# Gated mixing stage: two images at once, one on each half of the partitions

## The chip, the cores and the metric

One core of a Trainium2 chip runs the whole program. The metric is the device time of one execution in microseconds (us), the median of the runs shown. The engines are TensorE (PE; its weight loads are PEld), VectorE (DVE), ScalarE (ACT), GpSimd (POOL) and SyncE (SP), and 16 DMA engines serve the queues of SP, ACT and POOL. All data is fp32.

## The reference

The input x has 8 images of 64 channels and 256x256 pixels. Two layers follow each other, each a group normalisation, an operator and a residual addition. The first layer is the one that is changed here:

```python
def layer0(v, ...):                       # v = _gn(x), 32 groups of 2 channels
    y = einsum('bwhc,dc->bwhd', v, mlp1_w) + mlp1_b
    x1 = _shift1(y[..., :c])              # each quarter of the channels moved by one pixel: up, down, left, right
    x2 = _shift2(y[..., c:2 * c])         # the same with the directions exchanged
    x3 = sigmoid(batchnorm(v) * wbn) * v
    bar = softmax(mlp(sum(x1) + sum(x2)))           # two weights for each image and channel
    out = bar[:, 0] * x1 + bar[:, 1] * x2
    return (einsum('bwhc,dc->bwhd', out, mlp2_w) + mlp2_b) * x3
x = x + layer0(_gn(x), ...)
x = x + spectral(_gn(x), ...)             # 2-D real FFT, 32x32x2 modes mixed by complex 64x64 matrices, inverse FFT
```

## The kernel before

The program runs in stages, one after another. First come the statistics of x (0 to 336 us in the trace) and the preparation of small matrices. Then comes the mixing stage (378 to 1469 us), which computes x1 = x + layer0. A small normalisation step, the forward transform, the mixing of modes and the inverse transform with the residual addition follow.

In the mixing stage every image has its own four 64x64 matrices, one for each direction of shift (in `wall`, 4 x 64 columns on two halves of the partitions), and four numbers a channel (in `params`): scale and bias of the sigmoid, the mean, and the constant of the convolution. A matmul contracts over 128 partitions, so two shifts are taken at once: the tile `mix_x` (`XT`) holds the image's channels on partitions 0 to 63 as they are and on 64 to 127 moved by a row and a column. Reading it at one row and column for m=0 and at another for m=1 gives all four shifts with two matmuls.

One tile is 16 rows of one image, 17 rows of 257 elements in the buffer. There are 128 tiles (8 images of 16) and four buffers `XT`. For each tile:

- SP (lines 564, 567) loads the lower 9 rows to partitions 0 to 63 and the upper 9 to 64 to 127, in two DMAs. It waits for the matmuls (`conv_done`) and the sigmoid (`sig_done`) of the tile four before.
- DVE completes the two halves with two copies of 8 rows across the halves, `up` (line 686) and `down` (line 691).
- POOL (line 589) writes the edge column of each half, two small operations, once `down` has run (`doubled`, then `padded`).
- PE (line 617) runs 16 matmuls of 512 columns into one half of PSUM. Even and odd rows go to the two halves of the array's columns, so the results have rows of even parity on partitions 0 to 63 and of odd parity on 64 to 127.
- ACT subtracts the mean into `centred` (line 640), two operations of 64 partitions. In each odd tile DVE does the upper half (line 699). Then ACT forms the sigmoid into `gated` (line 648).
- DVE forms h = (psum + constant) * gate (line 721, `h_done`) and the output (h + 1) * centred with its sum into `mix_out` (line 730, `o_done`), of which there are two buffers.
- ACT issues the store of 1024 KB (line 661) and squares the output with a sum (line 666).

No scheduler is at work: each engine executes its list in the order of the code. DVE runs `up` of tile n+2, line 721 of tile n, `down` of n+2, line 730 of n, and line 699 of n+2 where n+2 is odd. ACT runs the gate of tile n+2 and then store and square of tile n.

## Time and profile before

| | us |
|---|---|
| median of 3 runs (lowest to highest) | 3148.63 (3142.68 to 3155.87) |
| the profiled execution | 3143.03 |
| its span, from the first to the last instruction | 3141.4 |
| mixing stage, 370 to 1469 us of the span | 1099 |
| forward transform, 1469 to 2060 | 591 |
| modes, 2060 to 2416 | 356 |
| inverse transform, 2416 to 3141 | 725 |

The stages don't overlap, so a change of the mixing stage is read from that stage alone, and the 1.6 us between span and time stay as they are. Over the whole span PE is busy 72%, DVE 64%, ACT 41% and POOL 24%. In the mixing stage DVE is busy 1001 of 1099 us, PE 936, ACT 891 and POOL 319. The views used are the groups of instructions by line, the instructions in order of time, busy time in chosen stretches with the share of the DMA engines, and durations line by line with least, median and greatest value.

### The profile page before, as it was taken

Reading aid. Unit: us, or ns where it says so; the run is one execution under the profiler, and the core shown is the slowest. Engines: PE = TensorE matmul, PEld = TensorE weight load, DVE = VectorE, ACT = ScalarE, POOL = GpSimd, SP = SyncE. Lnnn points to the kernel's source line nnn. Section 1 sums busy time; section 2 is a strip of 40 time slices with the busy share of each in tenths; the row PEclk is TensorE's granted clock in tenths of the full one; section 3 lists DMA queues with packets and bytes.
Section 4 is the critical chain, followed back from the end, with each engine's and each line's share of the span. In section 5 each row is a group of like instructions: output and inputs, shape, how many; then the busy total and the mean of one; then the engine's idle time right before and its main releaser. Section 6 shows DMA issues by size and latency. Waiting matters only on the chain. (4 is left out here: it accounts for less than half of the span.)

```text
span 3141.4 us, 38560 instructions
## 1 busy us (share of the span) xinstructions
PE 2248.2 (72%) x12960; PEld 1077.8 (34%) x12960; DVE 2023.4 (64%) x2317; ACT 1299.6 (41%) x1470; POOL 752.3 (24%) x477
## 2 busy tenths in 40 slices
PE   0000288888888888885999999945554898988874
PEld 0000123222323322221445444435553444444442
DVE  8999599989989998996665565620000454544442
ACT  1111188878888887885332232310000222212220
POOL 1000032332223232323655454500000111111111
PEclk9999899999999999998999999977787999998997
DMA  9999299999999999997877676569998999999999
GB/s 401 428 429 428 64 256 275 268 251 270 263 269 255 276 275 253 266 273 233 323 253 266 241 258 251 215 156 296 306 304 232 382 400 382 393 379 407 399 379 347
DMA packets 537810, 942.89 MB, mean 300 GB/s; under 512 B 16896, under 2 KB 459952, under 8 KB 493136
## 3 DMA queue, kind: packets, MB, share of 16 engines
q1 hardware_dynamic: 299264, 613.33, 62.3%
q10 hardware_dynamic: 202880, 192.95, 20.2%
q0 software_dynamic: 35536, 134.84, 11.2%
q8 instruction: 85, 1.39, 0.2%
q14 instruction: 45, 0.37, 0.0%
HBM read 647.46 MB, written 293.60 MB: 300 GB/s over the span
## 5 line engine op out<-in xcount | busy, mean ns | idle before, releaser
L617 PE MATMUL psum<-mix_x,wcur 128*64 128x512 f32 x4096 | 936.5, 613 | 154.5 <-POOL mix_x L589 135.9
L617 PEld LDWEIGHTS psum<-mix_x,wcur 128*64 128x64 f32 x4096 | 314.5, 139 | 775.9 <-issue 569.9
L1258 PE MATMUL psum<-tab_irow_icol_sign,inv_t 128*128 128x512 f32 x1024 | 495.6, 608 | 17.5 <-DVE inv_x L1305 15.4
L589 POOL TENSOR_TENSOR mix_x<-mix_x,one 64x17 f32<-64x17 f32 x256 | 318.7, 1245 | 755.1 <-DVE mix_x L691 747.6
L640 ACT ACTIVATE centred<-mix_x,pcur 64x2048 f32<-64x2048 f32 x192 | 384.5, 2003 | 206.9 <-POOL mix_x L589 190.9
L1076 POOL TENSOR_TENSOR fwd_diff<-x_tile 128x2048 f32<-128x2048 f32 x64 | 308.0, 4814 | 288.7 <-PE psum L868 255.6
L982 ACT ACTIVATE fwd_rows<-psum 128x512 f32<-128x512 f32 x256 | 152.3, 598 | 408.1 <-PE psum L868 384.1
L730 DVE SCALAR_TENSOR_TENSOR mix_out<-gated,centred 128x2048 f32<-128x2048 f32 x128 | 293.6, 2294 | 40.6 <-issue 37.3
L721 DVE SCALAR_TENSOR_TENSOR gated<-psum,pcur,gated 128x2048 f32<-128x2048 f32 x128 | 300.9, 2351 | 21.9 <-PE psum L617 20.2
L264 DVE BATCH_NORM_STATS2 stats<-stat_x 128x6 f32<-128x512 f32 x512 | 305.4, 684 | 13.6 <-DMA stat_x<-x 13.2
L1051 DVE COPY fwd_cols<-psum 128x136 f32<-128x136 f32 x512 | 154.4, 394 | 231.9 <-PE psum L879 230.9
L868 PE MATMUL psum<-fwd_sum,tab_ident_frow_fcol 128*64 128x512 f32 x512 | 281.2, 633 | 28.0 <-POOL fwd_diff L1076 18.2
L1286 ACT ACTIVATE inv_t<-psum 128x256 f32<-128x256 f32 x256 | 98.4, 385 | 477.6 <-PE psum L1249 477.6
L1121 PE MATMUL psum<-mode_w,mode_x 128*16 128x64 f32 x4096 | 170.0, 361 | 162.6 <-DMA mode_x<-modes_in 159.8
L868 PE MATMUL psum<-fwd_diff,tab_ident_frow_fcol 128*64 128x512 f32 x512 | 281.6, 634 | 0.0
L648 ACT ACTIVATE gated<-centred,pcur 128x2048 f32<-128x2048 f32 x128 | 268.4, 2097 | 11.2 <-DVE centred L699 2.9
L1305 DVE TENSOR_TENSOR inv_x<-inv_x,psum 128x1024 f32<-128x1024 f32 x128 | 155.7, 1221 | 175.6 <-PE psum L1258 142.3
L1305 DVE TENSOR_TENSOR x_tile<-x_tile,psum 128x1024 f32<-128x1024 f32 x128 | 156.2, 1221 | 166.9 <-PE psum L1258 159.1
L1258 PEld LDWEIGHTS psum<-tab_irow_icol_sign,inv_t 128*128 128x128 f32 x1024 | 199.6, 196 | 166.4 <-issue 147.1
L666 ACT ACTIVATE square<-mix_out 128x2048 f32<-128x2048 f32 x128 | 242.6, 1895 | 3.6 <-DVE mix_out L730 3.6
L296 PE MATMUL psum<-s_ones_dmask_spread_npix,w1d 128*64 128x128 f32 x1 | 0.4, 392 | 333.9 <-PEq L200 333.9
L1249 PE MATMUL psum<-tab_irow_icol_sign,inv_yy 128*128 128x256 f32 x512 | 159.7, 396 | 102.2 <-ACT inv_yy L1280 102.2
(183 smaller groups left out, 1948.6 us busy)
## 6 DMA issues: line engine op xcount, KB each, us to landing
x_tile<-x_scratch SPq DMA_DIRECT2D x184, 1024.0 KB, 7.7
mix_x<-x SPq DMA_DIRECT2D x240, 576.0 KB, 8.2
stat_x<-x SPq DMA_DIRECT2D x64, 2048.0 KB, 13.2
x_scratch<-mix_out ACTq DMA_DIRECT2D x128, 1024.0 KB, 9.0
inv_x<-x_scratch SPq DMA_DIRECT2D x64, 1024.0 KB, 11.6
out<-x_tile POOLq DMA_DIRECT2D x64, 1024.0 KB, 17.6
out<-inv_x POOLq DMA_DIRECT2D x64, 1024.0 KB, 15.6
mode_w<-L_conv_w_imag ACTq DMA_DIRECT2D x16, 2048.0 KB, 21.2
```

Source lines behind the costliest of these rows:

```text
L264: last = nc.vector.bn_stats(stats[:, at:at + 6], XT[t % NX][:, q * 512:(q + 1) * 512])
L589: last = nc.gpsimd.tensor_tensor(XT[n % NX][h, :, to], XT[n % NX][h, :, of], one[h, :], ALU.mult)
L617: last = nc.tensor.matmul(bank(k * 4 + q, 512, C, par * C), wcur[j][:, m * C:(m + 1) * C], XT[n % NX][:, r0:r0 + 3:2, m:m + W], start=(m = ...
L640: last = nc.scalar.activation(XC[n % NX][h, :].rearrange("p (r w) -> p r w", w=W), XT[n % NX][h, 1:MR:2, 1 - half:1 - half + W], ACT.Ident ...
L648: nc.scalar.activation(G[n % NX][:, :], XC[n % NX][:, :], ACT.Sigmoid, bias=pcur[j][:, 1:2], scale=pcur[j][:, 0:1]).then_inc(sig_done, 1)
L666: nc.scalar.activation(SQ[:, :], XO[k][:, :], ACT.Square, accum_out=sqs[:, bass.ds(i * NI + n, 1)]).then_inc(sq_done, 1)
L721: nc.vector.scalar_tensor_tensor(out=G[n % NX][:, :], in0=psum[:, k * SC:(k + 1) * SC], scalar=pcur[j][:, 3:4], in1=G[n % NX][:, :], op0=A ...
L730: nc.vector.scalar_tensor_tensor(out=XO[k][:, :], in0=G[n % NX][:, :], scalar=1.0, in1=XC[n % NX][:, :], op0=ALU.add, op1=ALU.mult, accum_ ...
L868: last = nc.tensor.matmul(bank(n % 2, 512, C, par * C), frow[:, par, :], ED[G0 % 2][par][:, 2 * cp:2 * cp + 2, :], start=True, stop=True)
L1076: nc.gpsimd.tensor_tensor(ED[G0 % 2][1][:, :, :], XW[G0 % NX][:, 0, :, :], XW[G0 % NX][:, 1, :, :], ALU.subtract).then_inc(diff_done, 1)
L1258: last = nc.tensor.matmul(bank(n % 2 * 2 + a), TS[n % 2][:, a * P:(a + 1) * P], icol, start=True, stop=True)
L1305: nc.vector.tensor_tensor(xw, xw, psum[:, n % 2 * 1024:n % 2 * 1024 + 1024] .rearrange("p (a k) -> p a k", a=2), ALU.add).then_inc(added, 1)
```

## The change

The mixing stage takes two images at once. A tile is now 8 rows of an image pair, one image on partitions 0 to 63 and the other on 64 to 127; there are again 128 tiles. One DMA of 128 partitions loads 10 rows a tile (1280 KB) into `mix_u` (`U`). For the matmuls each image must still stand on both halves, one of them moved by a row and a column (`SHIFT`, 259 elements). A second buffer `mix_v` (`V`) takes the second image: ACT copies it from the upper half of U to the lower half of V (`low`), POOL copies it moved from the upper half of U to the upper half of V (`up`), and then DVE overwrites the upper half of U with the first image, moved (`double`). POOL's edge columns are one operation, done straight after the load. The centring is one DVE operation of 128 partitions and comes before `double`, since it needs both images. The output is written in place into `gated` (four buffers instead of two), the square's unused elementwise result goes into `centred`, and the scratch tensor x1 is laid out by image pair. The number of matmuls and their sizes stay. With pairs, the loop over the tiles has 2 passes of 64 tiles instead of 4 of 32.

```diff
-PITCH = W + 1
+PITCH = W + 2
...
-        x1 = nc.dram_tensor("x1_scratch", (B, H, C, W), F32, kind="Internal").ap()
+        x1 = nc.dram_tensor("x1_scratch", (NQ, H, 2, C, W), F32, kind="Internal").ap()
...
                             sp.wait_ge(conv_done, i * NI + n + 1)
-                            sp.wait_ge(sig_done, i * NI + n + 1)
-                            r0 = t * MR - 1
-                            lo = max(r0, 0)
-                            sp.dma_start(xt[0:C, lo - r0:MR // 2 + 1, 1:W + 1],
-                                         x_rows[ch, lo:r0 + MR // 2 + 1, :]).then_inc(loaded[n % NX], 16)
-                            hi = min(r0 + MR + 2, H)
-                            sp.dma_start(xt[C:P, MR // 2:hi - r0 - 1, 0:W],
-                                         x_rows[ch, r0 + 1 + MR // 2:hi, :]).then_inc(loaded[n % NX], 16)
+                            r0 = t * SP_ - 1
+                            lo, hi = max(r0, 0), min(r0 + OWN, H)
+                            sp.dma_start(u[:, lo - r0:hi - r0, 1:W + 1],
+                                         x_rows[pair, lo:hi, :]).then_inc(loaded[n % NX], 16)
...
+                    def pad(i, n, up_before):
+                        pool.wait_ge(loaded[n % NX], loaded_by(i, n))
+                        pool.wait_ge(up_done, up_before)
+                        u = rows_of(U[n % NX])
+                        nc.gpsimd.tensor_tensor(u[:, :, 0:W + 2:W + 1], u[:, :, 1:W + 1:W - 1], one[:, :, :],
+                                                ALU.mult).then_inc(padded, 1)
+                    def up(i, n):
+                        pool.wait_ge(padded, i * NI + n + 1)
+                        pool.wait_ge(conv_done, i * NI + n + 1)
+                        k = TAPS * PITCH - 1
+                        nc.gpsimd.tensor_copy(V[n % NX][C:P, 0:k], U[n % NX][C:P, SHIFT:SHIFT + k]).then_inc(up_done, 1)
...
+                    def low(i, n):
+                        act.wait_ge(padded, i * NI + n + 1)
+                        act.wait_ge(conv_done, i * NI + n + 1)
+                        k = TAPS * PITCH
+                        nc.scalar.activation(V[n % NX][0:C, 0:k], U[n % NX][C:P, 0:k], ACT.Copy).then_inc(low_done, 1)
...
                     def body(i, final):
                         for n in range(NI):
                             if not (final and n + 2 >= NI):
+                                low(i, n + 2)
                                 gate(i, n + 2)
-                            act.wait_ge(o_done, i * NI + NX + n + 1)
+                            act.wait_ge(o_done, i * NI + n + 1)
...
+                    def centre(i, n):
+                        dve.wait_ge(loaded[n % NX], loaded_by(i, n))
+                        dve.wait_ge(sq_done, i * NI + n + 1)
+                        nc.vector.tensor_scalar(XC[n % NX][:, :].rearrange("p (r w) -> p r w", w=W),
+                                                rows_of(U[n % NX])[:, 1:SP_ + 1, 1:W + 1],
+                                                pcur[j][:, 4:5], None, ALU.add).then_inc(xc_done, 1)
+                    def double(i, n):
+                        dve.wait_ge(xc_done, i * NI + n + 1)
+                        dve.wait_ge(low_done, i * NI + n + 1)
+                        dve.wait_ge(up_done, i * NI + n + 1)
+                        k = TAPS * PITCH - 1
+                        nc.vector.tensor_copy(U[n % NX][C:P, 0:k], U[n % NX][0:C, SHIFT:SHIFT + k]).then_inc(doubled, 1)
...
-                                up(i, n + 2)
+                                centre(i, n + 2)
...
-                                down(n + 2)
+                                double(i, n + 2)
                             dve.wait_ge(h_done, i * NI + 2 + n + 1)
-                            dve.wait_ge(stored[k], i * (NB * 16) + n // 2 * 16 + 16)
-                            dve.wait_ge(sq_done, i * NI + n + 1)
-                            nc.vector.scalar_tensor_tensor(out=XO[k][:, :], in0=G[n % NX][:, :],
+                            nc.vector.scalar_tensor_tensor(out=G[n % NX][:, :], in0=G[n % NX][:, :],
```

The order on DVE in the loop, before, for one even and one odd tile (`mix_x` is the loaded tile, `gated` and `centred` as above):

```order
L686 COPY mix_x0<-mix_x0 64x8x256 [waits mix_loaded0]
L719 REGISTER_ALU
L721 SCALAR_TENSOR_TENSOR gated2<-psum,pcur0,gated2 128x2048 [waits mix_sig,mix_conv]
L691 COPY mix_x0<-mix_x0 64x8x256
L730 ISA [waits mix_sq,mix_stored0,mix_h]
L730 SCALAR_TENSOR_TENSOR mix_out0,sums<-gated2,centred2 128x2048
```

And with the change, for two tiles, where `mix_v_low` and `mix_v_up` are the semaphores of ACT's and POOL's copies:

```order
L697 TENSOR_SCALAR centred0<-mix_u0,pcur0 128x2048 [waits mix_sq,mix_loaded0]
L725 SCALAR_TENSOR_TENSOR gated2<-psum,pcur0,gated2 128x2048 [waits mix_sig,mix_conv]
L707 COPY mix_u0<-mix_u0 64x2321 [waits mix_v_up,mix_v_low,mix_xc]
L732 SCALAR_TENSOR_TENSOR gated2,sums<-gated2,centred2 128x2048 [waits mix_h]
L697 TENSOR_SCALAR centred1<-mix_u1,pcur0 128x2048 [waits mix_sq,mix_loaded1]
L725 SCALAR_TENSOR_TENSOR gated3<-psum,pcur0,gated3 128x2048 [waits mix_sig,mix_conv]
L707 COPY mix_u1<-mix_u1 64x2321 [waits mix_v_up,mix_v_low,mix_xc]
L732 SCALAR_TENSOR_TENSOR gated3,sums<-gated3,centred3 128x2048 [waits mix_h]
```

Two copies became one, which now waits for ACT and POOL; the centring moved to the front of the tile; the last operation of a tile no longer waits for a store. On ACT, before:

```order
L640 ACTIVATE centred0<-mix_x0,pcur0 64x2048 [waits mix_o,mix_padded]
L640 ACTIVATE centred0<-mix_x0,pcur0 64x2048
L648 ACTIVATE gated0<-centred0,pcur0 128x2048 [waits mix_xc]
L660 REGISTER_ALU
L661 ISA [waits mix_o]
L661 DMA x1_scratch<-mix_out0 128x8x256
L666 ISA [waits mix_sq]
L666 ACTIVATE square,sqs<-mix_out0 128x2048
```

And with the change:

```order
L667 DMA x1_scratch<-gated1 128x8x256 [waits mix_o]
L670 ACTIVATE centred1,sqs<-gated1 128x2048
L642 ACTIVATE mix_v0<-mix_u0 64x2322 [waits mix_conv,mix_padded]
L652 ACTIVATE gated0<-centred0,pcur0 128x2048 [waits mix_stored0,mix_sq,mix_xc]
L667 DMA x1_scratch<-gated2 128x8x256 [waits mix_o]
L670 ACTIVATE centred2,sqs<-gated2 128x2048
```

The copy for V stands behind the square of the tile three before, and that square behind the `o_done` that DVE gives at the end of each tile. On POOL, with the change (before, it had only the edge operations, each pair waiting for `mix_doubled`):

```order
L593 COPY mix_v3<-mix_u3 64x2321 [waits mix_conv,mix_padded]
L585 TENSOR_TENSOR mix_u0<-mix_u0,one 128x10x2 [waits mix_v_up,mix_loaded0]
L593 COPY mix_v0<-mix_u0 64x2321 [waits mix_conv,mix_padded]
L585 TENSOR_TENSOR mix_u1<-mix_u1,one 128x10x2 [waits mix_v_up,mix_loaded1]
```

The edge operation now waits for the load itself, and a copy of 2321 elements follows each.

## Rows read from the trace of the kernel before

**Rows 1.** Busy time in stretches: us, engines busy (instructions), granted clock, DMA share, GB/s.

```profile
500.00:1000.00 500.00, 432.12 (x1884) 145.94 (x1882) 458.70 (x335) 409.76 (x266) 145.09 (x118) 0.96 1.05 264
...
640.00:660.00 20.00, 16.33 (x69) 5.40 (x63) 19.06 (x15) 17.45 (x11) 6.38 (x6) 0.91 1.09 258
660.00:680.00 20.00, 16.56 (x68) 5.29 (x69) 12.84 (x9) 11.25 (x9) 4.78 (x3) 0.91 0.77 195
```

**Rows 2.** Groups by line: count | busy us, mean ns | idle before, releaser.

```profile
L640 ACT ACTIVATE centred<-mix_x,pcur 64x2048 f32<-64x2048 f32 x192 | 384.5, 2003 | 206.9 <-POOL mix_x L589 190.9 <-issue 15.1
...
L721 DVE SCALAR_TENSOR_TENSOR gated<-psum,pcur,gated 128x2048 f32<-128x2048 f32 x128 | 300.9, 2351 | 21.9 <-PE psum L617 20.2
L730 DVE SCALAR_TENSOR_TENSOR mix_out<-gated,centred 128x2048 f32<-128x2048 f32 x128 | 293.6, 2294 | 40.6 <-issue 37.3 <-DMA x_scratch<-mix_out 0.7
...
L691 DVE COPY mix_x<-mix_x 64x2048 f32<-64x2048 f32 x128 | 156.8, 1225 | 4.0
L686 DVE COPY mix_x<-mix_x 64x2048 f32<-64x2048 f32 x128 | 156.3, 1221 | 23.3 <-DMA mix_x<-x 14.9 <-issue 4.0
...
L982 ACT ACTIVATE fwd_rows<-psum 128x512 f32<-128x512 f32 x256 | 152.3, 598 | 408.1 <-PE psum L868 384.1 <-issue 23.7
...
L699 DVE TENSOR_SCALAR centred<-mix_x,pcur 64x2048 f32<-64x2048 f32 x64 | 82.4, 1288 | 2.1
...
L1148 ACT ACTIVATE mode_y<-psum 128x1024 f32<-128x1024 f32 x16 | 16.4, 1024 | 320.2 <-PE psum L1121 306.7 <-DVE mode_y L1172 13.5
```

**Rows 3.** DVE in order of time: start us, us, instruction [idle before].

```profile
407.22 0.08 DVE L730 DVE_READ_ACCUMULATOR mix_out<-gated,centred  x1
...
1464.09 0.08 DVE L730 DVE_READ_ACCUMULATOR mix_out<-gated,centred 128x1 f32 x1
```

**Rows 4.** ACT in order of time, steady state and the stage's last tile.

```profile
713.93 1.90 ACT L666 ACTIVATE square<-mix_out 128x2048 f32<-128x2048 f32 x1
715.73 0.19 ACT L666 ACTIVATION_READ_ACCUMULATOR square<-mix_out  x1
715.82 1.99 ACT L640 ACTIVATE centred<-mix_x,pcur 64x2048 f32<-64x2048 f32 x1
...
1464.20 0.38 ACTq L661 DMA_DIRECT2D x_scratch<-mix_out  x1
1464.63 1.91 ACT L666 ACTIVATE square<-mix_out 128x2048 f32<-128x2048 f32 x1 [3.59 <-DVE mix_out L730]
```

**Rows 5.** Single lines: ns min/median/max, first and last start; last row: stores' landing, us.

```profile
L589 POOL TENSOR_TENSOR mix_x<-mix_x,one x256: 222/1209/2357, 390.0 to 1451.0; 64x17 f32<-64x17 f32 x128
...
L1076 POOL TENSOR_TENSOR fwd_diff<-x_tile x64: 4504/4617/6501, 1485.3 to 2042.9; 128x2048 f32<-128x2048 f32 x64
...
DMA to landing us min/median/max: 4.5/9.0/12.1
```

**Rows 6.** Stretches with loads alone, then with a store alone.

```profile
405.00:415.00 10.00, 7.33 (x36) 2.35 (x34) 9.85 (x8) 6.27 (x4) 6.22 (x4) 1.00 1.13 204
415.50:417.50 2.00, 1.83 (x10) 0.61 (x10) 1.95 (x3) 2.00 (x3) 0.43 (x1) 1.00 1.08 380
```

**Rows 7.** PE in order of time, blocks of matmuls [idle before].

```profile
692.45 14.01 PE L617 MATMUL psum<-mix_x,wcur 128*64 128x512 f32 x64 [1.35 <-POOL mix_x L589]
...
860.38 15.69 PE L617 MATMUL psum<-mix_x,wcur 128*64 128x512 f32 x64 [2.16 <-POOL mix_x L589]
...
885.32 7.11 PE L617 MATMUL psum<-mix_x,wcur 128*64 128x512 f32 x32 [1.53 <-POOL mix_x L589]
```

**Rows 8.** DVE and POOL in order of time around 1615 us, forward transform.

```profile
1616.66 4.90 DVE L1006 TENSOR_TENSOR fwd_sum<-x_tile 128x2048 f32<-128x2048 f32 x1
...
1614.89 4.52 POOL L1076 TENSOR_TENSOR fwd_diff<-x_tile 128x2048 f32<-128x2048 f32 x1 [1.84 <-PE psum L868]
```

**Rows 9.** SP in order of time: the load's issue after the block that starts at 692.45.

```profile
706.65 0.60 SPq L564 DMA_DIRECT2D mix_x<-x  x1
```

**Rows 10.** The page, span in 40 equal slices: GB/s of the DMA engines.

```profile
GB/s 401 428 429 428 64 256 275 268 251 270 263 269 255 276 275 253 266 273 233 323 253 266 241 258 251 215 156 296 306 304 232 382 400 382 393 379 407 399 379 347
```

More of the change, by code:

```diff
@@ L81, in constants @@
     put("spread", spread.reshape(P, -1))
+    both = np.stack([0.5 * ((p[:, None] // C == d) & (c[:, None] // 2 == c[None, :] // 2)) for d in range(2)], 1)
+    put("both", both.reshape(P, -1))
     put("sign", np.stack([np.where(p < C, 1.0, -1.0)] * 2, 1))
@@ L574, in _ @@
                                              ).then_inc(loaded[n % NX], 16)
-                    for k in range(2):
-                        sp.wait_ge(stored[k], B * NB // 2 * 16 + 16)
+                    for k in range(NX):
+                        sp.wait_ge(stored[k], ITER * NI // NX * 16 + 16)
                 @block.gpsimd
                 def _(pool):
-                    nc.gpsimd.memset(one[:, :], 1.0).then_inc(one_set, 1)
+                    nc.gpsimd.memset(one[:, :, :], 1.0).then_inc(one_set, 1)
@@ L582, in _ @@
                     pool.wait_ge(one_set, 1)
-                    def pad(i, n):
-                        pool.wait_ge(doubled, i * NI + n + 1)
-                        for half, to, of in ((0, 0, 1), (1, W, W - 1)):
-                            h = slice(half * C, (half + 1) * C)
-                            last = nc.gpsimd.tensor_tensor(XT[n % NX][h, :, to], XT[n % NX][h, :, of],
-                                                           one[h, :], ALU.mult)
-                        last.then_inc(padded, 1)
@@ new lines, in up @@
+                    def up(i, n):
[3 more added lines that the diff above has]
+                        nc.gpsimd.tensor_copy(V[n % NX][C:P, 0:k], U[n % NX][C:P, SHIFT:SHIFT + k]).then_inc(up_done, 1)
+                    for n in range(3):
+                        pad(0, n, n)
+                        up(0, n)
+                    pad(0, 3, 3)
+                    def body(i, final):
+                        for n in range(NI):
+                            if not (final and n + 3 >= NI):
+                                up(i, n + 3)
+                            if not (final and n + 4 >= NI):
+                                pad(i, n + 4, i * NI + n + 4)
@@ L634, in gate @@
                             act.wait_ge(batch_ready, i * 2 + n // NB + 1)
-                        act.wait_ge(padded, i * NI + n + 1)
-                        act.wait_ge(o_done, i * NI + n + 1)
-                        for half in range(1 if split(n) else 2):
-                            h = slice(half * C, (half + 1) * C)
-                            last = nc.scalar.activation(
-                                XC[n % NX][h, :].rearrange("p (r w) -> p r w", w=W),
-                                XT[n % NX][h, 1:MR:2, 1 - half:1 - half + W],
-                                ACT.Identity, bias=pcur[j][h, 4:5])
@@ L703, in _ @@
                     dve.sem_inc(h_done, 2)
-                    dve.sem_inc(o_done, NX)
                     take(0, 0)
@@ L745, in program @@
         with ph:
-            T = table(ph, ["group", "ident"])
+            T = table(ph, ["both", "ident"])
             sv = sb(ph, "norm2_values", [P, 10, B])
@@ L751, in _ @@
                 def _(sp):
-                    for n in ("group", "ident"):
+                    for n in ("both", "ident"):
                         sp.dma_start(*T[n]).then_inc(n2_tab, 16)
@@ L762, in _ @@
                     pe.wait_ge(n2, 2)
-                    nc.tensor.matmul(bank(0, 2 * B), T["group"][0], sv[:, 2:4, :].rearrange("p a b -> p (a b)"),
-                                     start=True, stop=True).then_inc(n2, 1)
+                    for d in range(2):
+                        last = nc.tensor.matmul(psum[:, d * 1024:d * 1024 + 2 * NQ], T["both"][0][:, d * P:(d + 1) * P],
+                                                sv[:, 2, :], start=True, stop=True)
+                    last.then_inc(n2, 1)
                 @block.scalar
@@ L786, in _ @@
                     dve.wait_ge(n2, 5)
-                    v.scalar_tensor_tensor(out=sv[:, 6, :], in0=bank(0, 2 * B)[:, B:], scalar=EPS, in1=sv[:, 5, :],
+                    v.scalar_tensor_tensor(out=sv[:, 6, :], in0=sv[:, 8, :], scalar=EPS, in1=sv[:, 5, :],
                                            op0=ALU.add, op1=ALU.subtract).then_inc(n2, 1)
```

148 lines of the change are left out of this document (67 added, 81 removed).

## The prediction

> **What bounds the kernel now.** The change touches one stage, so I read that stage first as busy time in stretches: between 500 and 1000 us DVE is busy 458.70 of 500 us, PE 432.12, ACT 409.76 [rows 1]. DVE comes closest to full. The DMA engines' share is 1.05, so they too have next to nothing left. Then the groups by line give DVE's work for one tile: 2351 + 2294 ns for the two long operations, 1221 + 1225 ns for the two copies, and 1288 ns for the centring in every second tile, 644 a tile [rows 2]. That is 7.74 us. The end of the first and of the last output lie at 407.30 and 1464.17 us [rows 3], so the 127 tiles between them took 1056.87 us, 8.32 us each. The difference, 0.58 us a tile, goes into DVE's waits: line 730 stood idle 40.6 us, line 721 21.9, line 686 23.3 [rows 2], some before the steady state, and into the gaps between instructions. Some of it is the turn of the loop: around 660 us DVE is busy only 12.84 of 20 us where 19.06 is usual [rows 1], about 6 us lost, at three turns.
>
> **What goes and comes on each engine.**
>
> DVE loses a copy and half a centring of 64 partitions. It gets one centring of 128 partitions (1.29 us, since the time goes by elements in a partition) and one copy of 2321 elements. A copy of 2048 takes 1.22; at its rate for the additional 273 elements, 1.22 x 273/2048 = 0.16 at most, it is 1.38. The sum: 1.29 + 2.35 + 1.38 + 2.30 + 0.12 for gaps = 7.44 us. If DVE remained the bound, 0.88 us a tile would be gained, 112 us in all.
>
> ACT has three operations of 2.0 us in two tiles for centring now and gets one copy of 2322 elements instead. Its nearest rows are the same kind at 2048 elements, 2.00 us, and the slope between the PSUM copies of 512 and 1024 elements, (1024 - 598)/512 = 0.83 ns an element [rows 2], which makes 2.00 + 0.23 = 2.23. With the PSUM copies' base, 1.02 + 1298 x 0.00083 = 2.10. I take 2.2.
>
> **The new chain is what matters.** `low` of tile n+2 stands on ACT behind the square of tile n-1; that square waits for `o_done` of n-1; `double` of n+2 waits for `low`; and DVE's last operation of tile n stands behind `double`. So each output needs the one before it through ACT. In the last tile of the stage ACT did wait for the output, and its square began 1464.63 - 1464.17 = 0.46 us later, with the store's issue of 0.38 between [rows 3, 4]. From square to the next ACT instruction is 1.89 (713.93 to 715.82) [rows 4]. The chain for one tile: 0.46 + 1.89 + 2.20 (low) + 0.05 (handover) + 1.41 (double with its gap) + 2.30 (output) = 8.31 us. That is above DVE's own 7.44, above PE's 6.9 (two tiles of matmuls in 14.01 us, less the 0.2 of the pipeline [rows 7]), and by chance it is what a tile takes today. The cheaper DVE list is thus covered by a wait of 0.9 us before `double`.
>
> **The load.** Today the stage's loads alone run at 204 GB/s with the DMA engines full, a store alone at 380, in pieces of the same 1 KB [rows 6]. The loads go to 64 partitions each, the store comes from 128. The new load goes to 128. Its rate isn't shown: from below 204, from above 380. I take 350, since the pieces are alike and the partitions are those of the store. 1.31 MB then take 3.7 us instead of 1.18 MB in 5.8. The shortest landing of a store of 1.05 MB is 4.5 us [rows 5], of which 2.8 are data; so the new load lands 1.7 + 0.2 (SP's issue is 0.60, not 0.38 [rows 9]) + 3.7 = 5.6 us after its issue. DMA share falls to about (3.7 + 2.8)/8.3 = 78%.
>
> **POOL's copy and the shared port.** The trace has no POOL copy. A two-input operation of 17 elements takes 222 ns at least and one of 2048 4504 [rows 5], 2.11 ns an element. A copy reads one stream: half the slope makes 0.2 + 2321 x 1.055 = 2.65 us. From above, with the whole slope, 5.1. From below ScalarE's 2.2. I take 2.5, near the one-stream value. The Trainium skill, GPSIMD Engine Reference, section 3.1, puts a simple body at 1.03 cycles an element at 1.2 GHz, from which I estimate 2.0 us and a dispatch; no row here shows that, and by it T below would be 8.45 and the time 3163.
>
> Does it cost DVE anything? A DVE operation with two SBUF inputs that started 1.77 us into a POOL operation took 4.90 us, not 2.28, and ended 2.1 us after POOL's end (1614.89 + 4.52 = 19.41; 1616.66 + 4.90 = 21.56) [rows 8]. So the two engines exclude each other there. POOL's edge operations show the other direction: least 222 ns, greatest 2357, which is one whole output operation [rows 5]. The Trainium skill, SBUF — State Buffer, section "Who interferes with whom", states this as an exclusive lock for copies, scalar operations and two-input operations from SBUF, held for the whole instruction; the trace agrees with the 4.90.
>
> So per tile the centring, `double` and the output exclude POOL, and only line 725's 2.4 us and the 0.9 us wait are free for 0.25 + 2.5 us of POOL work. It fits only if it comes at the right time. Tile n+4's load is issued when the matmuls of n end: 14.20 us after the start of two of them [rows 7, 9], so 7.3 after `double` of n. It lands 5.6 later. Edge and handovers take 0.4, the copy 2.5: POOL is through 15.8 us after `double` of n. `double` of n+2 should start 2T - 1.4 after it. This is undisturbed only if 2T is 17.2 or more, T 8.6. With T = 8.31 it would collide by 0.6 us, so the port sets T to 8.6. A copy that just misses its window is worse: it starts behind the output operation and delays the next centring by its whole length, 2.5 us less the 0.9 of slack. And PE's idle time grows to T - 6.9 = 1.7 us at every tile. After 1.35 and 1.53 us of idle the clock stayed at 2.4 GHz (two tiles in 14.01, one in 7.11), after 2.16 it fell to 1.2 for a while (15.69, 1.7 more) [rows 7], and each such fall sends the next load out 1.7 us later, into the port's busy time. I add 0.05 a tile for both: **T = 8.65**.
>
> **Sum.** 127 x (8.65 - 8.32) = +42. Two of three turns of the loop go, with today's 6 us in the old 8.32 each; the remaining one isn't in my 8.65: +6. The first tile: its load lands 2 to 3 us sooner: -3. `take` has twice the instructions half as often: 0. The other stages read x1 in pieces of 8 KB as before, at twice the pitch (128 KB); the statistics read x at a pitch of 256 KB at 401 to 429 GB/s, nothing slower than the inverse stage's 379 to 407 [rows 10], so 0. Sum +45 on the profiled execution's 3143 = 3188. The median of the runs lies 5.6 above that execution, within the runs' spread of 13; I leave 3187.
>
> **The rivals.**
> 1. *No collision*: the load lands in 5.2 or the POOL copy takes 2.1. Then the ACT chain alone holds, T = 8.3, and the time is 3143 - 2 + 6 - 3 = 3144, no change. For it: landing plus copy need to be only 0.6 us shorter than I take. Against it: spread of landings (4.5 to 12.1 for stores). Chance 0.26.
> 2. *The chain is shorter*: ScalarE's copy at 1.9 and the store's issue hidden, T = 7.9 to 8.1: 127 x (7.9 - 8.32) = -53, or -28, and +3 as above, 3093 to 3118. Down to DVE's own 7.44 it would be 3034. Chance 0.13.
> 3. *POOL's copy costs as much as a two-input operation*, 5.1 us: 2T = 7.3 + 5.6 + 0.4 + 5.1 + 1.4, T = 9.9: +201 and +3, 3347. Chance 0.05.
> 4. *The load stays at 204 GB/s*: 6.4 us for it and 2.8 for the store fill the DMA engines for 9.2 us a tile: +112 and +3, 3258. Chance 0.05.
> 5. *DVE's copy of 2321, an odd count, runs at one element a cycle* like the output operation: 2294 x 2321/2048 = 2.6, 1.2 more in the chain, T = 9.5: +150 and +3, 3296. The Trainium skill, VectorE: DVE Perf Modes, section "Mode 2×_2P", allows the fast mode for odd counts that are equal on both sides, as here; no row shows an odd one. Chance 0.04.
>
> **How the numbers follow.** The forecast has 0.47; its own range runs from T = 8.45 (3163) to T = 9.3 (3270), as misses and falls of the clock are rare or common. A measurement of this kernel can tell about 0.5%, 16 us. Faster by that: rival 2 and a little of 1, 0.15. Within: most of 1 and the forecast's lower end, 0.30. Slower: 0.55. The range 3120 to 3290 leaves out the lower part of 2 and the upper cases, 0.2 together.
>
> **What would show it.** Right: DVE waits before line 707, about 0.9 us and more each time, for ACT's line 642 (with rival 1 for it alone) and for POOL's line 593; ACT waits for line 732 before each square; some of the lines 697 or 707 show durations of over 2 us, or gaps before them, where POOL's line 593 overlaps; DMA share well under 1. Wrong: outputs 7.5 us apart with no wait before 707; a full DMA share; line 707 at 2.6 us throughout; line 593 at over 4.

## The result, and the profile after

The changed kernel takes 3224.24 us (median of 4 runs, 3219.48 to 3228.28) against 3148.56 before on the same chip (4 runs, 3142.68 to 3155.87): a ratio of 1.0239, 95% interval 1.0213 to 1.0264. It is slower, as forecast, and inside the range; but it lost 76 us where the forecast had 38. The profiled execution has a span of 3222.2 us against 3141.4, 80.8 us more, where the forecast's sum for it was +45.

First the stretch of [rows 1], after (us, busy time of PE, PEld, DVE, ACT, POOL, granted clock, DMA share, GB/s):

```profile
500.00:1000.00 500.00, 415.40 (x1804) 128.06 (x1798) 436.22 (x293) 350.21 (x226) 158.77 (x113) 0.96 0.81 265
```

Nothing is full any more. DVE fell from 458.70 to 436.22 us, and the DMA engines from 1.05 to 0.81 at the same 265 GB/s: the 128-partition load does as much in less of their time. Yet fewer tiles come out of it. The accumulator reads that end the first and the last output, to set beside [rows 3], DVE in order of time:

```profile
405.65 0.08 DVE L732 DVE_READ_ACCUMULATOR gated<-gated,centred 128x1 f32 x1
...
1529.66 0.08 DVE L732 DVE_READ_ACCUMULATOR gated<-gated,centred 128x1 f32 x1
```

1124.0 us for 127 tiles, 8.85 each, where it was 8.32. What the engines wait for (engine, line and releaser: us in total, times, longest), 420 to 1500 us:

```profile
POOL mix_u L585 <- DMA mix_u<-x: 717.3, 120, 11.5
...
ACT centred L670 <- DVE gated L732: 320.0, 121, 4.7
...
PE psum L625 <- DVE mix_u L707: 187.9, 99, 3.9
DVE mix_u L707 <- issue: 137.1, 110, 1.6
```

This is the chain of the prediction: the square waits for the output at nearly every tile, line 707 waits 1.25 us each time, PE waits for line 707. The profile names "issue" before 707, that is, no releaser; the order of time shows what it is. These rows of DVE, ACT and POOL hold the end of an undisturbed tile and a whole disturbed one (start us, us, instruction, idle before):

```profile
718.73 0.08 DVE L732 DVE_READ_ACCUMULATOR gated<-gated,centred 128x1 f32 x1
718.73 1.28 DVE L697 TENSOR_SCALAR centred<-mix_u,pcur 128x2048 f32<-128x2048 f32 x1
719.93 2.34 DVE L725 SCALAR_TENSOR_TENSOR gated<-psum,pcur,gated 128x2048 f32<-128x2048 f32 x1
723.52 1.36 DVE L707 COPY mix_u<-mix_u 64x2321 f32<-64x2321 f32 x1 [1.25 <-issue]
724.92 4.09 DVE L732 SCALAR_TENSOR_TENSOR gated<-gated,centred 128x2048 f32<-128x2048 f32 x1
728.95 0.07 DVE L732 DVE_READ_ACCUMULATOR gated<-gated,centred 128x1 f32 x1
...
718.85 0.38 ACTq L667 DMA_DIRECT2D x_scratch<-gated  x1
719.27 1.91 ACT L670 ACTIVATE centred<-gated 128x2048 f32<-128x2048 f32 x1 [2.12 <-DVE gated L732]
721.09 0.18 ACT L670 ACTIVATION_READ_ACCUMULATOR centred<-gated 128x1 f32 x1
721.30 2.14 ACT L642 ACTIVATE mix_v<-mix_u 64x2322 f32<-64x2322 f32 x1
...
723.66 3.20 POOL L593 COPY mix_v<-mix_u 64x2321 f32<-64x2321 f32 x1
```

Line 707 starts at 723.52, 0.08 after ACT's copy ends at 723.44: it waited for ACT. The links from start to start are 0.54 us from the accumulator read to the square, 2.03 from there to `low`, 2.22 to `double` and 1.40 to the output, whose own accumulator read starts 2.22 later in an undisturbed tile: 8.41 us. POOL's copy starts at 723.66, 0.14 after `double` did, and shows 3.20 us instead of 2.12; the output behind it shows 4.09 instead of 2.29 and ends 2.2 us after POOL. So a wait for the port does not stand as idle time in this profile. It is inside the duration of the operation that waits. The extremes of each line say the same (ns min/median/max):

```profile
L707 DVE COPY mix_u<-mix_u x128: 1362/1366/3317, 389.1 to 1516.5; 64x2321 f32<-64x2321 f32 x128
...
L732 DVE SCALAR_TENSOR_TENSOR gated<-gated,centred x128: 2291/2293/4093, 403.4 to 1527.4; 128x2048 f32<-128x2048 f32 x128
...
L593 POOL COPY mix_v<-mix_u x128: 2117/2118/4158, 386.0 to 1503.5; 64x2321 f32<-64x2321 f32 x128
```

Of the 127 distances between outputs the last two are short (4.60 and 4.95 us), 56 are under 8.46, most of these 8.40 or 8.41, and 69 are longer, up to 10.94. Most of the lengthening is in `double`: 54 of its 128 rows are more than 0.1 us above the shortest, against 12 of the centring and 4 of the output. A collision reaches PE too. Behind one in which line 707 took 2.96 us:

```profile
708.13 0.72 PE L625 MATMUL psum<-mix_u,wcur 128*64 128x512 f32 x1 [2.91 <-DVE mix_u L707]
...
708.64 1.06 PE L625 MATMUL psum<-mix_u,wcur 128*64 128x512 f32 x1
...
712.02 0.59 PE L625 MATMUL psum<-mix_u,wcur 128*64 128x512 f32 x1
```

After 2.91 us of idle time the matmuls take 1.06 us, the clock's lower level of 1.2 GHz (granted on average 0.57 from 708 to 712 us), and from 712.02 on 0.59 at 2.4 GHz again (granted 1.00). The next load is issued at 717.09, 9.0 us after the end of this line 707, where it is 7.3 without a fall of the clock. The loads land so (us from issue, min/median/max):

```profile
DMA to landing us min/median/max: 5.6/6.4/14.2
```

The first output came 1.6 us sooner. Behind the loop the span grew by another 15 us, against the prediction's nothing: 11.3 of them between the first and the last sum of the forward transform (576.0 us after, 564.7 before), 2.5 in the normalisation and 2.5 in the modes, less 1 in the rest.

```profile
L1006 DVE TENSOR_TENSOR fwd_sum<-x_tile x64: 2268/2280/4903, 1485.2 to 2049.9; 128x2048 f32<-128x2048 f32 x64
```
```profile
L1009 DVE TENSOR_TENSOR fwd_sum<-x_tile x64: 2268/2279/4906, 1553.3 to 2129.3; 128x2048 f32<-128x2048 f32 x64
```

The first row is the kernel before, the second the kernel after. The duration of these operations did not change.

### The profile page after: what moved, and what is told of

It is laid out like the page before. It is cut to its first block and busy times, and to the rows that moved or that the text cites. A ratio compares the mean times of both kernels' runs of the same rounds, so it can differ in the third digit from the quotient of the medians.

```text
span 3222.2 us, 37513 instructions
## 1 busy us (share of the span) xinstructions
PE 2265.2 (70%) x12962; PEld 1059.9 (33%) x12962; DVE 2021.8 (63%) x2252; ACT 1207.3 (37%) x1406; POOL 795.4 (25%) x475
## 5 line engine op out<-in xcount | busy, mean ns | idle before, releaser
L625 PE MATMUL psum<-mix_u,wcur 128*64 128x512 f32 x2048 | 943.0, 617 | 212.1 <-DVE mix_u L707 211.9
L625 PE MATMUL psum<-mix_v,wcur 128*64 128x512 f32 x2048 | 943.0, 617 | 0.0
L625 PEld LDWEIGHTS psum<-mix_u,wcur 128*64 128x64 f32 x2048 | 278.9, 141 | 863.7 <-issue 547.9
L670 ACT ACTIVATE centred<-gated 128x2048 f32<-128x2048 f32 x128 | 244.9, 1913 | 340.1 <-DVE gated L732 340.1
L707 DVE COPY mix_u<-mix_u 64x2321 f32<-64x2321 f32 x128 | 221.5, 1731 | 145.5 <-issue 140.9
L593 POOL COPY mix_v<-mix_u 64x2321 f32<-64x2321 f32 x128 | 307.4, 2402 | 8.2
L732 DVE SCALAR_TENSOR_TENSOR gated<-gated,centred 128x2048 f32<-128x2048 f32 x128 | 300.6, 2349 | 4.0
L642 ACT ACTIVATE mix_v<-mix_u 64x2322 f32<-64x2322 f32 x128 | 273.7, 2139 | 35.1 <-POOL mix_u L585 32.0
L625 PEld LDWEIGHTS psum<-mix_v,wcur 128*64 128x64 f32 x2048 | 279.3, 141 | 0.0
```

The costliest lines, as they stand in the source:

```text
L593: nc.gpsimd.tensor_copy(V[n % NX][C:P, 0:k], U[n % NX][C:P, SHIFT:SHIFT + k]).then_inc(up_done, 1)
L625: last = nc.tensor.matmul(bank(k * 4 + q, 512, C, e * C), wcur[j][:, e, m * C:(m + 1) * C], taps[e][:, r0:r0 + 2, m:m + W], start=(m == 0) ...
L642: nc.scalar.activation(V[n % NX][0:C, 0:k], U[n % NX][C:P, 0:k], ACT.Copy).then_inc(low_done, 1)
L670: nc.scalar.activation(XC[n % NX][:, :], G[n % NX][:, :], ACT.Square, accum_out=sqs[:, bass.ds(i * NI + n, 1)]).then_inc(sq_done, 1)
L732: nc.vector.scalar_tensor_tensor(out=G[n % NX][:, :], in0=G[n % NX][:, :], scalar=1.0, in1=XC[n % NX][:, :], op0=ALU.add, op1=ALU.mult, ac ...
```

## The experiments

There are twelve kernels, each timed against the kernel before on the same chip; all but e6 and e12 are made from the changed kernel. Those of the mixing loop come first. The time of a tile is the distance from first to last output over 127; the last two distances, 4.60 and 4.95 us in the changed kernel and in most of its variants, have no work for a later tile between them.

**1. Is it the port?** GpSimd's copy is cut to 128 elements a row, and GpSimd fills `mix_v` with zeros once at the start. The kernel leaves out nearly all of that copy and so the inputs that it brings.

```
-                        k = TAPS * PITCH - 1
+                        k = 128
```

> Of the changed kernel, GpSimd's copy of each tile (line 593) is cut from 2321 elements a row to 128; the rest of the upper half of mix_v keeps zeros that GpSimd writes once at the stage's start, so the taps of odd rows lack their inputs. What is left out is nearly all of GpSimd's work, and nothing else moves. Theory A (the loop's 8.85 us a tile is a chain of 8.40 us through ScalarE and VectorE, lengthened by 0.45 us a tile where VectorE waits for the shared port while GpSimd copies): the VectorE copies of line 707 come back to 1.36 us each from a mean of 1.73, and T to 8.40, so 127 x 0.45 = 57 us less, about 3167 us. Rival B (the port is not it; the late load and the chain alone set 8.85): no change, about 3224 us.

Measured: 3160.1 us, ratio 1.0036 (1.0024 to 1.0048), 8.37 us a tile. The `double` copy, line 709 here, is no longer drawn out:

```profile
L709 DVE COPY mix_u<-mix_u x128: 1362/1364/1486, 391.5 to 1457.2; 64x2321 f32<-64x2321 f32 x128
```

The port costs the change 61 us in the mixing loop (1062.6 us instead of 1124.0), 64 in the whole: 116 of the 127 distances here are 8.40 to 8.44. Theory A holds, B falls. What is left, 1062.6 us against 1056.9 in the kernel before, is the chain through ACT.

**2. The same without leaving work out.** GpSimd's copy of n+3 also waits for the centring of n+2, so that it begins beside line 725, which reads PSUM.

```
                         pool.wait_ge(conv_done, i * NI + n + 1)
+                        pool.wait_ge(xc_done, i * NI + n)
```

> Of the changed kernel, GpSimd's copy for tile n+3 waits besides for the centring of tile n+2, so that it starts beside the operation of line 725, which reads PSUM, and not beside the double copy. The computation is whole. Theory A (it is the overlap with the copies and the output that costs): GpSimd's 2.12 us fit beside the 2.34 us of line 725, line 707 falls from a mean of 1.73 us to 1.36 to 1.4, T to about 8.40: 57 us less, about 3167 us. Rival B (line 725 is hindered as well, or GpSimd's copy comes too late): 3224 us or more.

Measured: 3157.6 us, ratio 1.0033 (1.0016 to 1.0050), 8.36 us a tile. The copy lines of DVE and POOL (ns min/median/max), whole kernel:

```profile
L708 DVE COPY mix_u<-mix_u x128: 1362/1364/1365, 388.9 to 1454.5; 64x2321 f32<-64x2321 f32 x128
```
```profile
L594 POOL COPY mix_v<-mix_u x128: 2117/2120/3148, 385.8 to 1442.7; 64x2321 f32<-64x2321 f32 x128
```

No `double` is lengthened any more, and line 726, beside which the copy now runs, keeps its 2.345 us. Theory A again. One added wait gives back 62 us in the loop and 67 in the whole. It also ends the falls of TensorE's clock: granted 1.00 from 500 to 1000 us, where it was 0.96.

**3. Is it the chain through ScalarE?** ScalarE's copy of n+3 stands before its wait for output n, no longer behind the square. The copy of tile 2 is made ahead of the loop; that line is not in the cut.

```
-                                low(i, n + 2)
                                 gate(i, n + 2)
+                            if not (final and n + 3 >= NI):
+                                low(i, n + 3)
 
                             act.wait_ge(o_done, i * NI + n + 1)
```

> Of the changed kernel, ScalarE's copy of tile n+3 (line 642) stands before its wait for output n, behind the sigmoid of n+2, instead of behind the square of n. The computation is whole. Theory A (a chain output, square, low copy, double copy, output carries the loop): the link square to low copy to double copy leaves the chain, VectorE is bound by its own list of 1.28 + 2.34 + 1.36 + 2.29 us and gaps, 7.45 us a tile, plus whatever the port collisions with GpSimd add: T between 7.45 and 8.4, so 57 to 178 us less than 3224: 3046 to 3167 us, 3105 in the middle. Rival B (the load and GpSimd's copy of the upper half set the period, twice T = 17.6 us): T stays at 8.8, about 3220 us.

Measured: 3038.2 us, ratio 0.9642 (0.9606 to 0.9678), 7.36 us a tile. That is faster than either end I had given, because most distances are 7.18 or 7.19, where I had DVE's list at 7.45. Nearly all the rest are collisions, now rare and up to 11.2 us. GpSimd's copies show why they are rare:

```profile
L593 POOL COPY mix_v<-mix_u x128: 2117/3031/4151, 385.6 to 1310.3; 64x2321 f32<-64x2321 f32 x128
```

The median is 3.03 us, so now it is mostly GpSimd that waits, which costs the loop nothing. Rival B, that load and GpSimd's copy set the period whatever ACT does, falls: the load simply comes earlier when PE is earlier.

**4. Both, and the list of DVE alone.**

> Both edits of the two kernels beside it: ScalarE's copy one step earlier, GpSimd's copy held until the next centring is done. The computation is whole. Theory A: no ScalarE link in the chain and no collision, so VectorE's own list sets the pace, T = 7.45 to 7.7 us, 146 to 178 us less than 3224: 3046 to 3078 us, which would be below the kernel before (3149). Rival B (the load sets the period, T 8.8): about 3220 us. Rival C (the DMA engines, 0.81 busy at T = 8.85, so about 7.2 us of work a tile, slow their transfers down when less slack is left): T about 8, 3116 us.

Measured: 3009.8 us, ratio 0.9561 (0.9532 to 0.9590), 7.22 us a tile, with nothing left out. Its stretch and one tile of DVE:

```profile
500.00:1000.00 500.00, 487.42 (x2198) 151.63 (x2196) 492.91 (x362) 420.19 (x276) 245.21 (x138) 1.00 1.00 325
```
```profile
702.97 1.28 DVE L700 TENSOR_SCALAR centred<-mix_u,pcur 128x2048 f32<-128x2048 f32 x1
704.17 2.35 DVE L728 SCALAR_TENSOR_TENSOR gated<-psum,pcur,gated 128x2048 f32<-128x2048 f32 x1
706.54 1.36 DVE L710 COPY mix_u<-mix_u 64x2321 f32<-64x2321 f32 x1
707.94 2.29 DVE L735 SCALAR_TENSOR_TENSOR gated<-gated,centred 128x2048 f32<-128x2048 f32 x1
...
710.16 1.28 DVE L700 TENSOR_SCALAR centred<-mix_u,pcur 128x2048 f32<-128x2048 f32 x1
```

Next to no idle time is left: DVE is busy 492.91 of 500 us and goes round in 7.19. PE (487.42) and the DMA engines (1.00) are nearly full beside it. This is theory A, and faster than its range of 3046 to 3078 us, which had DVE's list at 7.45. The feared slowing by full DMA engines (C) shows only as a load that lands in 7.6 us at the median instead of 6.5 (the loads of 1280 KB), which is hidden. Of the two edits the early copy is worth most: alone it took the changed kernel from 3224 to 3038 us, and with it in place the held copy is worth 28 us more, not 67.

> Of the changed kernel, GpSimd's copy is cut to 128 of 2321 elements a row (so most of the odd-row taps' inputs are left out) and ScalarE's copy of n+3 stands before its wait for output n. With whole GpSimd copies the second edit alone gave 7.36 us a tile, and with the copies held beside line 725 it gave 7.22, of which VectorE is busy 7.2. Theory A (VectorE's own list is the bound, all that collisions still cost is 7.36 - 7.2): T = 7.20 to 7.22, so no faster than the held version: span 3000 to 3012 us, about 3010 us. Rival B (GpSimd's held copy still costs something, by its traffic or by line 707, which it lengthens a little): below 7.15, 3000 us or less.

Measured, with GpSimd's copy cut instead of held: 3010.5 us, ratio 0.9559 (0.9527 to 0.9590), 7.21 us a tile. Cutting gains nothing over holding, so with the copy held the port costs next to nothing; theory A.

**5. Does the copy's length act through a ring of two tiles?** The ring is the one behind the forecast's T: from `double` of a tile through its matmuls, the load that they release, its landing and GpSimd's copy, which still holds the port when `double` of two tiles later is due. Here GpSimd copies twice.

```
+                        nc.gpsimd.tensor_copy(V[n % NX][C:P, 0:k], U[n % NX][C:P, SHIFT:SHIFT + k]).then_inc(up_first, 1)
+                        pool.wait_ge(up_first, i * NI + n + 1)
                         nc.gpsimd.tensor_copy(V[n % NX][C:P, 0:k], U[n % NX][C:P, SHIFT:SHIFT + k]).then_inc(up_done, 1)
```

> Of the changed kernel, GpSimd makes its copy of each tile twice, one after the other, to the same place, 2.12 us more a tile; the computation is whole. Theory A (load, pad, GpSimd copy, double copy close a ring around two tiles: 2T = 7.3 + 6.4 + 0.35 + 2.12 + 1.4 = 17.6 us, which the second copy makes 19.7): T from 8.85 to about 9.9, 127 x 1.05 = 133 us more, about 3357 us. Rival B (GpSimd's copies cost only by the port collisions, 0.45 us a tile, which then double, and the copy's length is in no ring): T = 9.3, 3281 us. Rival C (there is slack for the second copy beside line 725): no change.

Measured: 3342.6 us, ratio 1.0621 (1.0584 to 1.0657), 9.75 us a tile, 9.83 without the stage's last two. Theory A's 9.86 is met on average; B's 9.3 isn't. But the tiles are uneven, 8.40 to 11.86 us, and PE's granted clock between 500 and 1000 us fell to 0.90 from 0.96, which neither theory held; so the average alone doesn't prove the ring. Consecutive DVE and POOL rows show collisions on both sides:

```profile
722.28 4.09 DVE L735 SCALAR_TENSOR_TENSOR gated<-gated,centred 128x2048 f32<-128x2048 f32 x1
726.31 0.08 DVE L735 DVE_READ_ACCUMULATOR gated<-gated,centred 128x1 f32 x1
726.31 3.14 DVE L700 TENSOR_SCALAR centred<-mix_u,pcur 128x2048 f32<-128x2048 f32 x1
...
721.02 3.21 POOL L594 COPY mix_v<-mix_u 64x2321 f32<-64x2321 f32 x1
724.29 4.07 POOL L596 COPY mix_v<-mix_u 64x2321 f32<-64x2321 f32 x1
```

The closer evidence for the ring is in the changed kernel itself. The accumulator reads of two outputs, eight tiles apart:

```profile
764.76 0.08 DVE L732 DVE_READ_ACCUMULATOR gated<-gated,centred 128x1 f32 x1
...
833.94 0.08 DVE L732 DVE_READ_ACCUMULATOR gated<-gated,centred 128x1 f32 x1
```

These eight tiles took 8.65 us each, every one between 8.44 and 8.85. All the loads behind them landed in 6.0 to 6.4 us, no output or centring is lengthened, and each `double` takes 1.40 to 1.80 us.

**6. Where do the forward transform's 11 us come from?** The first suspicion is the wider pitch of the intermediate image. It was put into the kernel before (e6, shown), and taken out of the kernel with both edits of experiment 4 (e8); in both, each store becomes two of 64 partitions.

```
-        x1 = nc.dram_tensor("x1_scratch", (B, H, C, W), F32, kind="Internal").ap()
+        x1 = nc.dram_tensor("x1_scratch", (B, H, 2, C, W), F32, kind="Internal").ap()
```

> The kernel before, with its first intermediate image laid out as the changed kernel has it, so that the rows of one image lie 128 KB apart in HBM and not 64 (the other half stays unused), and each store made as two of 64 partitions. The computation is whole. It asks where the 11 us come from that the changed kernel lost in the forward transform (sums from 1485.2 to 2049.9 us, 564.7, before; 576.0 after). Theory A (the wider pitch slows those loads): the same stretch takes 573 to 578 us here, the whole about 3157 us. Rival B (code and arrangement of the stage, or the run): 563 to 567 us, and the whole at 3149 to 3152 us.

> The changed kernel with ScalarE's copy one step earlier and GpSimd's copy held until the next centring is done (3009.8 us), and besides the intermediate image's rows back at a pitch of 64 KB, each store made as two of 64 partitions. The computation is whole. The forward stretch took 570.6 us in the kernel without the last edit. Theory A (the pitch costs 6 to 11 us there): 563 to 566 us and the whole about 3003 us. Rival B (it does not): 569 to 573 us, the whole 3010 us. A second store issue costs ScalarE 0.38 us a tile, of 1.15 us that it has idle before each square, so the mixing loop should stay at 7.2 us a tile.

Measured: 565.2 us between the sums with the wide pitch in the kernel before, against 564.7; 574.4 with the narrow one in the kernel with both edits, against 570.6. The pitch is not the cause; rival B both times, if 1.4 us above its range in the second. The times of the whole, 3179.8 and 3026.1 us, missed what I expected by some 29 and 16 us. Of these 23 and 7 arose in the mixing loop (8.50 us a tile for 8.32, 7.27 for 7.22). In both the store is in two parts, and I had called the second one hidden. But the pitch of the stores was changed too, to the wide one in e6 and to the narrow one in e8, so what the split alone costs isn't shown.

The waits of PE in the stretch, before and after (line and releaser: us, times, longest):

```profile
PE psum L900 <- issue: 6.6, 2, 3.5
```
```profile
PE psum L903 <- issue: 11.3, 4, 4.3
```

In order of time they stand at the stage's two turns of the loop, after:

```profile
1838.55 1.01 PE L903 MATMUL psum<-tab_ident_frow_fcol,fwd_cols 128*128 128x128 f32 x3 [3.60 <-issue]
1841.33 5.33 PE L903 MATMUL psum<-tab_ident_frow_fcol,fwd_cols 128*128 128x128 f32 x29 [1.78 <-issue]
1992.79 1.01 PE L903 MATMUL psum<-tab_ident_frow_fcol,fwd_cols 128*128 128x128 f32 x3 [4.28 <-issue]
1995.44 5.09 PE L903 MATMUL psum<-tab_ident_frow_fcol,fwd_cols 128*128 128x128 f32 x29 [1.65 <-issue]
```

A turn here is the place where the stage's loop jumps back to its start. Each of the two turns has a second stall, three matmuls behind the first. Before, there is one stall a turn:

```profile
1765.77 5.44 PE L900 MATMUL psum<-tab_ident_frow_fcol,fwd_cols 128*128 128x128 f32 x32 [3.45 <-issue]
```

The stalls together are 4.7 us longer than before (11.3 for 6.6), of the 11 us that the stage lost; 3.4 of these are the second ones. TensorE's busy time in the stage also rose, from 522.5 to 530.0 us, at a granted clock of 0.95 where it was 0.96. Part of that stands right behind the stalls: 29 matmuls take 5.33 us there, at a granted clock of 0.65, where 32 without a stall ahead take 3.74:

```profile
1773.60 3.74 PE L903 MATMUL psum<-tab_ident_frow_fcol,fwd_cols 128*128 128x128 f32 x32
```

TensorE's program for this stage is the same in both kernels, and in the kernel with the narrow pitch x1 lies in HBM as before; what differs is where the code lies, and it may be where the buffers lie on the chip. So the code alone was moved, by instructions that do nothing:

```
+                    for _ in range(16):
+                        pe.sem_inc(pe_pad, 1)
                     pe.sem_inc(row_done, 8)
                     pe.sem_inc(tr_done, 2)
```

> The kernel with ScalarE's copy earlier and GpSimd's held (3009.8 us), with 16 increments of an unused semaphore ahead of TensorE's work of the forward stage; the computation is whole. It asks after the 6 to 12 us that the forward stretch takes longer in all kernels with the change than in the two without. At each of the two turns of that stage's loop TensorE stands still for 3.1 to 3.7 us with no releaser; in the kernels with the change a second stall of 1.7 to 2.1 us follows three matmuls later. Theory A (where the loop's code lies decides whether a second piece of it has to be fetched): with the code moved on by 16 instructions the second stalls vanish, line 908's idle time on issue falls from 11.4 to about 7 us, and the forward stretch from 570.6 to about 567 us. Rival B (the stalls come from something else): 4 stalls, 11 us, as before. The whole: 3003 to 3010 us.

> The same with 48 increments, a larger move. Theory A: the number of stalls after a loop turn goes with the place of the code, so 2 or 4, 7 or 11 us, but not the same for all three paddings (0, 16, 48). Rival B: 4 stalls and 11 us for all three. The whole within 6 us of 3010 us.

Measured, with 16: 557.7 us between the sums, 12.9 less than the 570.6 without them; with 48: 557.4 us. The whole takes 2997.6 us, ratio 0.9550 (0.9527 to 0.9572), and 2995.6 us in a single run with 48. The ratio without them was 0.9561 (0.9532 to 0.9590), so of the 13 us in the stage the time of the whole shows only some 5, within the noise. Not only the second stalls are gone but all of them; line 909, PE's counterpart of 903 here, waits for data alone:

```profile
PE psum L909 <- DVE fwd_cols L1060: 3.4, 4, 0.9
```

I had expected the first stalls to stay, and 567 us. Rival B, four stalls as before, falls.

> The changed kernel with nothing but 16 increments of an unused semaphore ahead of TensorE's work of the forward stage; the computation is whole. Theory A (the 11 us that the changed kernel lost in the forward stage are stalls at the two turns of its loop that go with the place of the code): no stall with issue as its cause on line 903's successor, the stretch between the first and the last sum 576.0 to about 558 us, the whole 3224 to about 3207 us. Rival B (in this kernel it is something else): 570 us or more, 3218 us or more.

> The kernel before with the same 16 increments; the computation is whole. Theory A: what it has of the stalls (3.5 and 3.1 us) goes too, if 16 instructions are a fitting distance from its own place, and the stretch falls from 564.7 to about 558 us, the whole from 3149 to about 3142 us; with both kernels so padded the forward stage no longer differs, and of the 76 us between them some 65 to 68 are left, those of the mixing loop. Rival B (before, the place with 16 is a bad one, as it differs from kernel to kernel): 565 to 576 us and 3149 to 3160 us.

Measured: the changed kernel so padded takes 3207.8 us, ratio 1.0197 (1.0175 to 1.0219), with no stall and 560.3 us between the sums, against 576.0, as theory A had it. The kernel before, so padded, takes 3149.7 us, ratio 0.9995 (0.9977 to 1.0014), with 567.6 us and both stalls (3.3 and 4.3 us): theory A there falls, rival B holds. Sixteen instructions are a good distance from one starting point and not from another. Which piece of the machine stands behind the place of the code was not tried apart.

## Why the prediction was right in sign and short in size

**The chain.** Right: the cheaper DVE list was covered by ACT's wait for the output and DVE's wait for `low`. Its term was 8.31 us; it measured 8.41. The error is in the link from the square to the next ACT instruction, 2.03 for 1.89, of which the other links give back 0.04. The row of before had a plain successor; here 0.21 us pass between the start of the accumulator read and the start of `low`, not 0.09. 125 tiles x 0.10 = 12 us too little.

**The port.** Right in kind and in place; the tile's time went from 8.41 to 8.92 without the last two, 0.51 us, where I had 0.34: 21 us too little. Two terms in it were off in opposite directions. The load lands 6.4 us after its issue at the median (5.6 at least), not 5.6, and POOL's copy takes 2.12, not 2.5. With these, 2T = 7.3 + 6.4 + 0.35 + 2.12 + 1.4 = 17.6, T = 8.79. With the 6.2 us of the eight even tiles above it is 8.69, and they measured 8.65. What this formula leaves out are the tiles in which GpSimd's copy came later still and ran into the output or the next centring: 16 of 125, and they alone are 24 us longer than 8.41 each. That is 0.19 us a tile, for which I had added 0.05. The Trainium skill, SBUF — State Buffer, section "Who interferes with whom", says that the lock is held for the whole instruction and that an operation with at most one input from SBUF and outside the two-port modes stays out of it; the trace agrees with the output that shows 4.09 us for 2.29 and with line 725, whose first input comes from PSUM and which stays at 2.345 beside the copy. The Trainium skill, GPSIMD Engine Reference, section 3.1, had made the copy 2.0 us and a dispatch by my estimate; 2.12 agrees, and my 2.5 was 18% too long. The time worked out from the page, 3163, is off all the same: the landing was the larger error.

**The loop's turn and its end.** The turn was put at +6 us. The distances around it are 8.80, 8.41 and 8.85 us, no more than elsewhere: with the chain as the bound there was slack that hides it (in the kernel with both edits, which has no such slack, the distance at the turn is 9.99, for 7.19). And the last two outputs come 7.8 us sooner than 2 x 8.65. Together 14 us too much. So: 127 x 8.65 + 6 = 1104.6, + 12 + 21 - 14 = 1124, what was measured. My 48 us for the loop became 67 by errors that partly cancel: that the miss is no larger is in part luck. The first output came 1.6 us sooner, where I had 3.

**The other stages.** "The other stages ... so 0" was wrong by 15 us. I had asked only for the DMA's rates, and the pitch did prove harmless. I had not asked what happens to unchanged code behind a changed stage. 11 us of it are the forward transform, where the padded kernel takes back 16. The 2.5 us in the modes were not tried, nor the 2.5 in the normalisation, whose code the change did touch. So the profiled execution's +45 became +80.8: 19 us in the loop, 1.4 at the first output, 15 behind the loop. The sum was made on that execution, 3143 + 45 = 3188, and set down as 3187 for the median, which lay 5.6 above it; that alone made the forecast's 45 into 38.

**The rivals.** No collision (3144) is what the held copy makes of it: 3157.6, or 3150 without the 8 us that its forward transform takes longer (572.7 us). For the change as it was made it was wrong: POOL's copy did take the 2.1 us of its condition, but the landing was longer than I took and undid that. The shorter chain did not come by itself, but moving one ScalarE instruction gave it, and below the bound I had set: DVE's list is 7.19 us, not 7.44. I had added 0.12 for gaps, where the centring starts 0.08 before the output's row ends. The two-input price for POOL's copy (5.1 us) is refuted by 2.12, the load at 204 GB/s by a DMA share of 0.81, and the slow odd copy (2.6) by 1.36.

The signs that I named came in: waits before 707 (1.25 us each), before the square, durations over 2 us in 707, DMA share 0.81. Only their releaser reads "issue", and not ACT's line 642.

## What to carry to other kernels

Shortening the list of the busiest engine gives nothing where an instruction of another engine stands behind a wait for that list's own last result; look where each producer stands in its engine's order, and move it ahead of the wait. Where GpSimd copies within SBUF, give it a start that is tied to an operation of VectorE that reads PSUM, rather than to the landing of a load: one wait was worth 67 us here by itself and 28 once ScalarE's copy was early, and both edits together turned a loss of 2.4% into a gain of 4.4%. Before unchanged stages are put at nothing, look at the stalls with no releaser behind the turns of their loops: a few idle instructions ahead of such a loop took 13 to 16 us off that stage in two kernels with the change and nothing in the kernel before, so they have to be tried for each kernel.

## What the runs showed of the hardware that I had not expected

- A wait for the port that VectorE and GpSimd share shows no idle time in the profile; it lengthens the row of the operation that waits: 1.36 us to 3.32, 2.29 to 4.09, GpSimd's 2.12 to 4.16. Small operations are hit as well: a VectorE copy of 128 elements a row took 2.15 us instead of 0.25 beside GpSimd's copy (e2, at 755.86 us).
- TensorE stood still 3.1 to 4.3 us behind each turn of the forward transform's loop, and in all unpadded kernels with the change 1.6 to 2.5 us more three matmuls later, with no releaser. The number of stalls went from 4 to 0 with 16 or 48 idle instructions ahead of the loop in kernels with the change, and stayed at 2 with 16 in the kernel before.
- With the store of 128 partitions made as two of 64 and the pitch of x1 changed as well, the loop took 23 us more in 128 tiles in the kernel before, whose DMA share was 1.05, and 7 us more in the kernel with both edits.
- Loads and stores together moved 325 GB/s at a DMA share of 1.00 with loads into 128 partitions, and 264 at 1.05 with loads into 64.
